# Sixteen graph-network batches on one core: z of eleven batches turned on VectorE and moved by DMA instead of through TensorE

## The chip, the cores and the metric

One NeuronCore of a Trainium2 chip runs the whole program. The metric is the device time of one execution in microseconds (us); lower is better. Engines are named as the profile names them: PE (TensorE matmul), PEld (its weight loads), DVE (VectorE), ACT (ScalarE), POOL (GpSimd), SP (SyncE, which only issues DMAs here).

## What is computed

Sixteen batches `x[b]` of 512 nodes with 128 features go through a two-layer attention network and then through a third attention layer. All arithmetic is fp32. Cut to what matters:

```python
h = relu(layernorm(x))                              # 16 x 512 x 128
o1 = relu(h @ mlp1_w + mlp1_b)                      # 512 x 256 per batch
g1 = gat(o1, None, W_fc, a_fc)                      # attention over all 512 nodes
z = elu(g1) + o1                                    # the residual of the first layer
o2 = relu(z @ mlp2_w + mlp2_b)                      # 512 x 128
g2 = gat(o2, adj, W_hand, a_hand)
x = x + relu(elu(g2) + o2)
x = x + gat(relu(layernorm(x)), adj, W, a)

def gat(inp, adj, W, a):
    h = inp @ W
    e = leaky_relu(h @ a1 + (h @ a2).T)             # 512 x 512
    return elu(softmax(masked(e, adj)) @ h)
```

## The kernel before

**Tiling.** Nodes are cut into C = 4 chunks of 128. The network runs batch by batch, but the batches overlap: every engine has a list `ORDER[engine]` of steps such as `att1_2.7` (attention sums of layer 1, chunk 2, batch 7), which it works off in exactly that order. A step waits on semaphores for its inputs and for its buffers. TensorE's steps fill PSUM banks in rotation: filling number k uses bank k mod 8, and waits until the filling eight before it has been read (`free`, `read_by`).

**The steps of one batch, in the order of the data.** `mlp1_0`, `mlp1_1` (L1416) make o1 by features, that is with features on the partitions and the 512 nodes in the free dimension; ACT puts it into `o1_t` with the ReLU (L790). `h1_0` to `h1_3` (L1426) multiply it with `W_fc`, ACT copies the result to `ext` (L798). DVE finds a column maximum (`max1`, L1138), POOL takes it over the partitions (L732), DVE and ACT make the score factors (`args1`), a row of 512 scores is spread over the partitions (`row1`: DVE turns a 32-wide square, SP writes four small pieces to DRAM at L686 and loads them back as a broadcast at L695), and DVE makes four `prob` tiles of 128x512 (L1184). `att1_0` to `att1_3` (L1437) are the attention sums, one chunk of 128 target nodes each. For each, DVE takes the reciprocal of the row sum (L1250) and ACT scales it to `y` (L892); for each half of the batch ACT then applies exp twice (L911, L915) and DVE forms `u = max(y, min(e, 1))` = elu + 1 (L1265).

**The piece that the change touches.** `u` lies by nodes (nodes on the partitions, 256 features in the free dimension), but `mlp2` needs z by features. So TensorE's steps `z_0` and `z_1` turn it, four 128x128 transposes into one bank each (L1445), and DVE's steps `z_0` and `z_1` (L1272) compute `z_t = (bank - 1) + o1_t`. `mlp2` (L1455) multiplies `z_t` with `mlp2_w`, ACT applies bias and ReLU (L921).

```python
def z(b, f):                       # TensorE, twice per batch
    pe.wait_ge(*s1.u.at(b, 2))
    filled = free(f"z_{f}", b)
    for c in range(C):
        last = nc.tensor.transpose(filled[:, c * P:(c + 1) * P], gat1.u[:, c, f * P:(f + 1) * P], ident[:])
    last.then_inc(z_filled.sem, 1)
```

After `mlp2` come layer 2 (`h2` L1477, `max2`, `args2`, `row2`, `prob2` L859 and L1211, `att2` L1530, `turn_o2` L1538) and layer 3 (`turn2` L1496, `h3` L1477, `max3`, `args3`, `row3`, `prob3`, `att3` L1530). The last three batches (13, 14, 15) run several steps in halves. POOL only takes maxima over the partitions, 16 batches times 3 layers and one guard; it issues no DMA. `o1_t` has 3 buffers, `z_t` has 2.

## Time and profile before

| | us |
|---|---|
| median of 3 runs | 432.97 |
| lowest, highest | 431.36, 433.53 |
| span of the profiled execution | 429.0 |
| PE busy, its share | 411.1, 96% |
| PEld, DVE, ACT busy | 352.7, 357.8, 315.7 |
| POOL busy | 24.9 |

The profile shows one execution of the program and its span from the first to the last instruction. It has no separate time for that execution with what lies around the span; the runs' median is 4.0 us more than the span, the lowest run 2.4 us more. In the profile's rows one fp32 matmul of the program is two MATMUL records (`att1`, 4 matmuls, is "x8"; `att2`, 8 matmuls, is "x16"), and a transpose is one (`z_0` is "x4"). Line numbers are those of the kernel before unless said otherwise. The chain of waits starts from the last instruction and goes back, at each step to what released it; its rows give the share of the span by engine and line. Matmuls are pipelined, so the cost of a step on the chain is the time from its piece to the next piece, not the mean duration of one matmul.

### The profile page before, as it was taken

The page shows a single profiled execution, that of the slowest core. Times are in us where ns is not written, and L with a number is a line of the kernel's source. Part 1 is how long each engine was busy: PE and PEld are TensorE (multiplying, and loading weights), DVE is VectorE, ACT ScalarE, POOL GpSimd, SP SyncE. Part 2 cuts the span into 40 slices and gives each one's busy share as a digit, 9 for nine tenths or more (in the row PEclk, how much of TensorE's full clock was granted, in tenths as well). Part 3 has the DMA queues.
Part 4 walks back from the last instruction along what each step waited for, and adds up shares of the span by engine and source line. Part 5 has one row for each costly group of instructions (what it writes and reads, how often), then busy time and mean ns, then how long its engine had stood idle before and what let it go on. Part 6 is the DMA issues. An engine that isn't in the chain of part 4 may idle for free.

```text
span 429.0 us, 8704 instructions
## 1 busy us (share of the span) xinstructions
PE 411.1 (96%) x2544; PEld 352.7 (82%) x2544; DVE 357.8 (83%) x1226; ACT 315.7 (74%) x764; POOL 24.9 (6%) x53
## 2 busy tenths in 40 slices
PE   6999999999999999999999999999999999989782
PEld 4688779887898899797998788989879799869772
DVE  7786588878998898988898868979698899889974
ACT  2655659658796787786878688687867887799774
POOL 0000000000001000010100000100000000000000
PEclk9999999999999999999999999999999999999997
DMA  7854323123423142232222213222320122120001
GB/s 209 278 146 130 105 74 121 74 76 98 125 98 75 53 138 84 52 101 74 75 82 68 75 53 98 79 72 74 80 87 10 49 93 59 45 80 24 27 1 57
DMA packets 39461, 36.42 MB, mean 85 GB/s; under 512 B 4080, under 2 KB 30320, under 8 KB 39408
## 3 DMA queue, kind: packets, MB, share of 16 engines
q1 hardware_dynamic: 37408, 33.17, 26.1%
q10 hardware_dynamic: 2000, 2.63, 1.8%
q8 instruction: 23, 0.38, 0.4%
q14 instruction: 30, 0.25, 0.2%
HBM read 31.46 MB, written 4.32 MB: 83 GB/s over the span
## 4 chain that ended last, share of the span: by engine, by line
PE 87%; DVE 5%; ACT 3%; issue 2%; DMA 1%; SPq 0%; POOL 0%; ACTq 0%; DVEq 0%
PE bank L1530 24%; PE bank L1437 23%; PE bank L1426 13%; PE bank L1416 6%; PE bank L1477 6%; PE bank L1455 6%; PE bank L1445 3%; PE bank L1538 2%; PE bank L1496 1%; PE bank L1466 1%; DMA row<-row_scratch 1%; DVE stats L1036 1%; DVE u L1265 1%; ACT ext L826 1%; ACT e L911 1%
## 5 line engine op out<-in xcount | busy, mean ns | idle before, releaser
L1530 PEld LDWEIGHTS bank<-ext,prob 128*128 128x128 f32 x1024 | 119.6, 192 | 6.3 <-issue 4.9
L1530 PE MATMUL bank<-ext,prob 128*128 128x129 f32 x1024 | 122.1, 275 | 0.3 <-DVE prob L1207 0.2
L1437 PE MATMUL bank<-ext,prob 128*128 128x257 f32 x512 | 119.0, 380 | 0.0
L1437 PEld LDWEIGHTS bank<-ext,prob 128*128 128x128 f32 x512 | 94.8, 190 | 17.3 <-issue 4.5
L1211 DVE SCALAR_TENSOR_TENSOR prob<-prob,square,mask_t 128x512 f32<-128x512 f32 x98 | 70.6, 739 | 0.9 <-ACT prob L859 0.8
L1426 PE MATMUL bank<-wfc_sb,o_t 128*128 128x259 f32 x256 | 64.0, 382 | 0.4 <-ACT o_t L790 0.4
L859 ACT ACTIVATE prob<-row,square 128x512 f32<-128x512 f32 x78 | 54.1, 720 | 0.1
L1426 PEld LDWEIGHTS bank<-wfc_sb,o_t 128*128 128x128 f32 x256 | 46.3, 190 | 9.6 <-issue 4.5
L903 ACT ACTIVATE y<-bank,recip 128x128 f32<-128x128 f32 x128 | 39.3, 369 | 15.3 <-DVE recip L1257 14.2
L911 ACT ACTIVATE e<-y,minus_one 128x512 f32<-128x512 f32 (+1 forms) x70 | 47.7, 688 | 1.4
L1265 DVE SCALAR_TENSOR_TENSOR u<-e,y 128x512 f32<-128x512 f32 (+1 forms) x70 | 44.1, 638 | 4.2 <-issue 2.2
L732 POOL PARTITION_ALL_REDUCE fmax<-fmax_col x48 | 24.3, 514 | 389.1 <-DVE fmax_col L1138 389.1
L892 ACT ACTIVATE y<-bank,recip 128x256 f32<-128x256 f32 x64 | 29.5, 468 | 16.0 <-DVE recip L1250 15.6
L915 ACT ACTIVATE e<-e,minus_one 128x512 f32<-128x512 f32 (+1 forms) x51 | 35.5, 697 | 2.4
L798 ACT ACTIVATE ext<-bank 128x259 f32<-128x259 f32 x64 | 24.1, 382 | 12.6 <-PE bank L1426 10.6
L1184 DVE TENSOR_SCALAR prob<-row,square 128x512 f32<-128x512 f32 x64 | 32.8, 533 | 0.1
L1416 PE MATMUL bank<-normed_t,w_sb 128*128 128x512 f32 x64 | 32.1, 594 | 0.5 <-DVE normed_t L1097 0.5
L1455 PE MATMUL bank<-z_t,w_sb 128*128 128x512 f32 x64 | 30.2, 594 | 0.0
L790 ACT ACTIVATE o_t<-bank,vec_sb 128x512 f32<-128x512 f32 x32 | 21.7, 682 | 5.4 <-PE bank L1416 4.0
L836 ACT ACTIVATE square<-args 128x12 f32<-128x12 f32 x48 | 10.0, 211 | 18.0 <-DVE args L1159 11.5
L1272 DVE SCALAR_TENSOR_TENSOR z_t<-bank,o_t 128x512 f32<-128x512 f32 x32 | 21.6, 677 | 0.6 <-PE bank L1445 0.2
L826 ACT ACTIVATE ext<-bank,rstd 128x131 f32<-128x131 f32 x64 | 19.1, 378 | 3.2 <-PE bank L1477 2.2
(98 smaller groups left out, 499.1 us busy)
## 6 DMA issues: line engine op xcount, KB each, us to landing
row<-row_scratch SPq DMA_DIRECT2D x36, 256.0 KB, 3.3
moments_row<-moments_scratch SPq DMA_DIRECT2D x13, 512.0 KB, 3.8
x_in<-in_x SPq DMA_DIRECT2D x16, 256.0 KB, 5.3
x_res<-in_x SPq DMA_DIRECT2D x16, 256.0 KB, 4.6
out<-y_out SPq DMA_DIRECT2D x15, 256.0 KB, 3.9
normed<-in_x_t SPq DMA_DIRECT2D x14, 256.0 KB, 4.3
row_scratch<-square_t SPq DMA_DIRECT2D x144, 0.5 KB
adj_sb<-in_adj ACTq DMA_DIRECT2D x1, 1024.0 KB, 8.1
```

Source lines behind the costliest of these rows:

```text
L859: nc.scalar.activation(L.prob_of(b)[:, t], row_of(b, L), ACT.Copy, scale=L.buv[:, b.slot, 2, t:t + 1]).then_inc((s.scaled_first if t == 0 ...
L903: nc.scalar.activation(L.y[:, c], filled[:, e * (D + 3):e * (D + 3) + D], ACT.Copy, bias=1.0, scale=L.recip[:, b.slot, c:c + 1]).then_inc( ...
L911: nc.scalar.activation(L.e[:, r], L.y[:, r], ACT.Exp, bias=minus_one[:]).then_inc(s.exp.sem, 2 // parts)
L915: nc.scalar.activation(L.e[:, r], L.e[:, r], ACT.Exp, bias=minus_one[:]).then_inc(s.exp2.sem, 2 // parts)
L1184: nc.vector.tensor_scalar(gat1.prob_of(b)[:, t], gat1.row[:, b.slot], gat1.buv[:, b.slot, 2, t:t + 1], gat1.buv[:, b.slot, 1, t:t + 1], AL ...
L1211: nc.vector.scalar_tensor_tensor(out=p, in0=p, scalar=L.buv[:, b.slot, 1, t:t + 1], in1=mask_t[:, t], op0=ALU.max, op1=ALU.min).then_inc(s ...
L1265: nc.vector.scalar_tensor_tensor(out=L.u[:, r], in0=L.e[:, r], scalar=1.0, in1=L.y[:, r], op0=ALU.min, op1=ALU.max).then_inc(s.u.sem, 2 // ...
L1416: nc.tensor.matmul(filled[:], w1_sb[:, f * P:(f + 1) * P], normed_t[0][:, b.slot], start=True, stop=True).then_inc(o1_filled.sem, 1)
L1426: last = nc.tensor.matmul(filled[:, 0:H + 3], o1_t[:, b.of(O1_DEPTH), k, c * P:(c + 1) * P], wfc_sb[:, k], start=(k == 0), stop=(k == HT - 1))
L1437: last = nc.tensor.matmul(filled[:, 0:H + 1], gat1.targets(b, t, c), gat1.features_and_one(b, t), start=(t == 0), stop=(t == C - 1))
L1455: last = nc.tensor.matmul(filled[:], w2_sb[:, k], z_t[:, b.slot, k], start=(k == 0), stop=(k == HT - 1))
L1530: last = nc.tensor.matmul(filled[:, e * (D + 3):e * (D + 3) + D + 1], L.targets(b, t, c), L.features_and_one(b, t), start=(t == 0), stop=( ...
```

## The change

For batches 2 to 12 (`MOVED`), z takes another way:

1. TensorE's two `z` steps and DVE's two `z` steps are left out.
2. DVE has two new steps, `turnu_0` and `turnu_1`, each one instruction that turns 32x32 blocks of a half of `u` into `u_turned` (one buffer; the next batch's first `turnu` waits until the writes of the batch before have landed).
3. POOL has a new step `move`: four DMAs, one for each group of 32 partitions, write `u_turned` to a scratch tensor in DRAM, 512 KB per batch in runs of 128 elements (512 bytes).
4. POOL has a new step `move_in`: it waits until those four have landed, then issues one DMA of 128x2x512 elements that reads the scratch and **adds** it onto `o1_t` in place (`accum_op=ALU.add`).
5. `mlp2` reads `o1_t` instead of `z_t`. For the moved batches the 512 nodes lie in `o1_t` in another order, 4 blocks of 4 pieces of 32 nodes; ACT writes them so (`by_blocks`), `mlp2` reads them back in the natural order, in pieces of 32 columns.
6. The "-1" of elu is no longer subtracted by DVE. It goes into the bias: a new step `sums_w2`, once, computes the column sums of `mlp2_w` on TensorE (two matmuls with one column) and DVE subtracts them from `b2_sb`. The five other batches keep their transposes, and their DVE step is a plain add onto `o1_t`.
7. `z_t` is gone, `o1_t` has 4 buffers. Some semaphores that were not used are left out.
8. All five lists in `ORDER` are new.

The diff, cut to its core (the lists of `ORDER` are left out, except POOL's first lines):

```diff
-O1_DEPTH = 3
+O1_DEPTH = 4
+MOVED = tuple(range(2, 13))
...
     "gpsimd": """
-        max1.0 max1.1 max1.2 max2.0 max1.3 max2.1 max1.4 max1.5 max3.0 max2.2 max2.3 max3.1 max2.4 max2.5
+        max1.0 max1.1 max1.2 max2.0 max2.1 max1.3 move.2 move_in.2 max1.4 max1.5 move.3 move_in.3 max3.0 max2.2
+        move.4 max3.1 move_in.4 max2.3 move.5 move_in.5 max2.4 max2.5 max1.6 max1.7 max3.2 max3.3 max1.8 move.6
...
+        u_turned = sb("u_turned", [P, HT * ROWS, C, 32])
+        blocks_scratch = nc.dram_tensor("blocks_scratch", [2, HT * P * N], fp32, kind="Internal").ap()
-        z_t = sb("z_t", [P, 2, HT, N])
...
+        def by_blocks(tile):
+            return tile.rearrange("p (a c i) -> p c a i", a=ROWS, c=C)
...
+            def write_blocks(b):                                     # POOL, "move"
+                pool.wait_ge(*u_blocks.at(b, 2))
+                if b.n - 2 in MOVED:
+                    pool.wait_ge(*z_moved.two_back(b))
+                places = blocks_scratch[b.slot].rearrange("(f j a n) -> a j f n", f=HT * ROWS, j=32, a=ROWS)
+                for a in range(ROWS):
+                    pool.dma_start(places[a], u_turned[32 * a:32 * (a + 1)].rearrange("p f c i -> p f (c i)")).then_inc(
+                        blocks_written.sem(b), 16)
+
+            def add_blocks(b):                                       # POOL, "move_in"
+                pool.wait_ge(*blocks_written.landed(b))
+                pool.wait_ge(*s1.h_filled.at(b, C))
+                pool.dma_start(o1_t[:, b.of(O1_DEPTH)], blocks_scratch[b.slot].rearrange("(k p n) -> p k n", k=HT, p=P),
+                               accum_op=ALU.add).then_inc(z_moved.sem(b), 16)
...
-                nc.scalar.activation(o1_t[:, b.of(O1_DEPTH), f], bank_of(f"mlp1_{f}", b)[:], ACT.Relu,
-                                     bias=b1_sb[:, f:f + 1]).then_inc(o1_ready.sem, 1)
+                o1, filled = o1_t[:, b.of(O1_DEPTH), f], bank_of(f"mlp1_{f}", b)[:]
+                if moved(b):
+                    o1, filled = by_blocks(o1), filled.rearrange("p (c a i) -> p c a i", a=ROWS, c=C)
+                nc.scalar.activation(o1, filled, ACT.Relu, bias=b1_sb[:, f:f + 1]).then_inc(o1_ready.sem, 1)
...
+            def turn_blocks(b, part):                                # DVE, "turnu"
+                r = slice(part * C // 2, (part + 1) * C // 2)
+                dve.wait_ge(*s1.u.at(b, part + 1))
+                earlier = [n for n in MOVED if n < b.n]
+                if part == 0 and earlier:
+                    dve.wait_ge(*blocks_written.landed(Batch.nth(earlier[-1])))
+                nc.vector.transpose(u_turned[:, :, r].rearrange("p f c i -> p c f i"),
+                                    gat1.u[:, r].rearrange("p c (f i) -> p c f i", i=32)).then_inc(u_blocks.sem, 1)
...
-                nc.vector.scalar_tensor_tensor(out=z_t[:, b.slot, f], in0=bank_of(f"z_{f}", b)[:], scalar=-1.0,
-                                               in1=o1_t[:, b.of(O1_DEPTH), f], op0=ALU.add, op1=ALU.add).then_inc(
-                    z_ready.sem, 1)
+                o1 = o1_t[:, b.of(O1_DEPTH), f]
+                nc.vector.tensor_tensor(o1, bank_of(f"z_{f}", b)[:], o1, ALU.add).then_inc(z_ready.sem, 1)
...
             def mlp2(b):                                             # TensorE
-                pe.wait_ge(*z_ready.at(b, HT))
+                pe.wait_ge(*(z_moved.landed(b) if moved(b) else z_ready.at(b, HT)))
                 filled = free("mlp2", b)
                 for k in range(HT):
-                    last = nc.tensor.matmul(filled[:], w2_sb[:, k], z_t[:, b.slot, k],
+                    z = o1_t[:, b.of(O1_DEPTH), k]
+                    last = nc.tensor.matmul(filled[:], w2_sb[:, k], by_blocks(z) if moved(b) else z,
                                             start=(k == 0), stop=(k == HT - 1))
```

**What the new order does, at two places.** The first is TensorE around batch 4. Before, from `h3_0.1` to `mlp2.4`; L1445 are the `z` transposes, first those of batch 4 and between them `att1_2.5` (L1437), and the last row is `mlp2.4`:

```order
L1477 MATMUL bank<-wl_sb,normed_t 128x131 x4
L1477 MATMUL bank<-whand_sb,o_t 128x131 x4
L1416 MATMUL bank<-normed_t,w_sb 128x512
L1437 MATMUL bank<-ext,prob 128x257 x8
L1416 MATMUL bank<-normed_t,w_sb 128x512
L1445 MATMUL bank<-ident,u 128x128 x4
L1437 MATMUL bank<-ext,prob 128x257 x4
L1445 MATMUL bank<-ident,u 128x128 x4
L1530 MATMUL bank<-ext,prob 128x129 x8
L1437 MATMUL bank<-ext,prob 128x257 x4
L1426 MATMUL bank<-wfc_sb,o_t 128x259 x2
L1455 MATMUL bank<-z_t,w_sb 128x512 x2
```

After, from `mlp2.3` (first row) to `mlp2.4` (last row). In the changed kernel L1518 is `mlp2`, L1499 `att1`, L1561 `turn2`, L1542 `h2` or `h3`, L1595 `att3`, L1478 `mlp1`. Just ahead of the first row stand the four `att1` steps of batch 4 and the four transposes of `row3.0`:

```order
L1518 MATMUL bank<-o_t,w_sb 128x512 x2
L1561 MATMUL bank<-ident,normed 128x128 x4
L1499 MATMUL bank<-ext,prob 128x257 x8
L1542 MATMUL bank<-wl_sb,normed_t 128x131 x4
L1542 MATMUL bank<-whand_sb,o_t 128x131 x2
L1499 MATMUL bank<-ext,prob 128x257 x4
L1542 MATMUL bank<-whand_sb,o_t 128x131 x2
L1499 MATMUL bank<-ext,prob 128x257 x4
L1595 MATMUL bank<-ext,prob 128x129 x8
L1478 MATMUL bank<-normed_t,w_sb 128x512
L1595 MATMUL bank<-ext,prob 128x129 x8
L1518 MATMUL bank<-o_t,w_sb 128x512 x2
```

The transposes are gone. `mlp2.4` comes after `att1_3.5` and both `att3` steps of batch 0.

The second place is POOL in the changed kernel, from `max2.3` (first row) to `move_in.8` (last row); L744 is a maximum over the partitions, L754 the four writes of a `move`, L761 the adding DMA of a `move_in`. Before, POOL's list was maxima alone:

```order
L744 ISA fmax<-fmax_col 128x1
L754 DMA blocks_scratch<-u_turned 32x8x128 x4
L761 DMA o_t<-blocks_scratch 128x2x512
L744 ISA fmax<-fmax_col 128x1 x7
L754 DMA blocks_scratch<-u_turned 32x8x128 x4
L761 DMA o_t<-blocks_scratch 128x2x512
L744 ISA fmax<-fmax_col 128x1 x2
L754 DMA blocks_scratch<-u_turned 32x8x128 x4
L761 DMA o_t<-blocks_scratch 128x2x512
L744 ISA fmax<-fmax_col 128x1 x4
L754 DMA blocks_scratch<-u_turned 32x8x128 x4
L761 DMA o_t<-blocks_scratch 128x2x512
```

Maxima now stand behind the waits of `move` and `move_in` on the same engine; ahead of `move.7` (the third L754) are `max2.6` and `max3.4`, and ahead of `move.8` are `max1.9`, `max3.5`, `max2.7` and `max1.10`.

## Rows read from the trace of the kernel before

**Rows 1.** The page: busy time of each engine, share of the span, instructions

```profile
PE 411.1 (96%) x2544; PEld 352.7 (82%) x2544; DVE 357.8 (83%) x1226; ACT 315.7 (74%) x764; POOL 24.9 (6%) x53
```

**Rows 2.** The page: chain of waits, shares of the span by engine and line

```profile
PE 87%; DVE 5%; ACT 3%; issue 2%; DMA 1%; SPq 0%; POOL 0%; ACTq 0%; DVEq 0%
PE bank L1530 24%; PE bank L1437 23%; PE bank L1426 13%; PE bank L1416 6%; PE bank L1477 6%; PE bank L1455 6%; PE bank L1445 3%; PE bank L1538 2%; PE bank L1496 1%; PE bank L1466 1%; DMA row<-row_scratch 1%; DVE stats L1036 1%; DVE u L1265 1%; ACT ext L826 1%; ACT e L911 1%
```

**Rows 3.** Windows: us, busy PE, PEld, DVE, ACT, POOL, then granted clock, DMA share, GB/s

```profile
0.00:30.00 30.00, 25.46 (x118) 19.55 (x119) 23.57 (x119) 13.74 (x32) 1.11 (x6) 1.00 0.74 219
30.00:60.00 30.00, 30.00 (x147) 23.92 (x146) 21.17 (x85) 19.27 (x45) 1.27 (x3) 1.00 0.37 107
...
330.00:360.00 30.00, 30.00 (x198) 26.87 (x197) 26.83 (x88) 23.30 (x60) 1.81 (x5) 1.00 0.19 59
360.00:390.00 30.00, 28.21 (x193) 24.74 (x192) 25.68 (x82) 26.70 (x63) 2.22 (x4) 1.00 0.19 57
390.00:429.00 39.00, 27.40 (x227) 25.30 (x225) 30.03 (x100) 27.14 (x73) 1.05 (x3) 0.93 0.10 30
```

**Rows 4.** The chain of waits from 190 us on: start us, us, what

```profile
190.29 1.73 PE bank L1437 x8
...
192.90 0.86 PE bank L1416 x2
...
194.63 0.44 PE bank L1445 x4
...
198.65 1.79 PE bank L1455 x4
...
202.17 0.89 PE bank L1477 x8
203.07 0.88 PE bank L1426 x4
...
207.44 1.78 PE bank L1530 x16
```

**Rows 5.** Groups of instructions: busy us, mean ns of one | idle before

```profile
L1265 DVE SCALAR_TENSOR_TENSOR u<-e,y 128x512 f32<-128x512 f32 x58 | 39.3, 684 | 4.0 <-issue 2.2 <-ACT e L915 1.3 <-ACT e L911 0.6
...
L1184 DVE TENSOR_SCALAR prob<-row,square 128x512 f32<-128x512 f32 x64 | 32.8, 533 | 0.1
L915 ACT ACTIVATE e<-e,minus_one 128x512 f32<-128x512 f32 x45 | 32.5, 722 | 2.2
...
L892 ACT ACTIVATE y<-bank,recip 128x256 f32<-128x256 f32 x64 | 29.5, 468 | 16.0 <-DVE recip L1250 15.6 <-DVE u L1265 0.2
...
L1272 DVE SCALAR_TENSOR_TENSOR z_t<-bank,o_t 128x512 f32<-128x512 f32 x32 | 21.6, 677 | 0.6 <-PE bank L1445 0.2
...
L1445 PE MATMUL bank<-ident,u 128*128 128x128 f32 x128 | 18.5, 273 | 1.7 <-DVE u L1265 1.7
...
L1129 DVE TENSOR_SCALAR normed<-x,meanvar 128x128 f32<-128x128 f32 x64 | 14.3, 282 | 0.7
...
L1369 PE MATMUL bank<-vec_sb,turned_w 128*128 128x3 f32 x8 | 1.0, 242 | 0.0
```

**Rows 6.** DMA issues on SP from 238 us on: start us, us, what

```profile
238.29 1.28 SPq L663 DMA_DIRECT2D moments_scratch<-moments_t  x4
241.31 0.35 SPq L668 DMA_DIRECT2D moments_row<-moments_scratch  x1
...
249.97 1.06 SPq L675 DMA_DIRECT2D x_res<-in_x  x1
```

**Rows 7.** DMA issues: KB each, median us from issue to landing

```profile
moments_row<-moments_scratch SPq DMA_DIRECT2D x13, 512.0 KB, 3.8
...
out<-y_out SPq DMA_DIRECT2D x15, 256.0 KB, 3.9
...
adj_sb<-in_adj ACTq DMA_DIRECT2D x1, 1024.0 KB, 8.1
```

More of the change, by code:

```diff
@@ L66 @@
+        move.4 max3.1 move_in.4 max2.3 move.5 move_in.5 max2.4 max2.5 max1.6 max1.7 max3.2 max3.3 max1.8 move.6
+        move_in.6 max2.6 max3.4 move.7 move_in.7 max1.9 max3.5 max2.7 max1.10 move.8 move_in.8 max3.6 move.9 max2.8
+        move_in.9 move.10 max2.9 move_in.10 max1.11 max3.7 max2.10 max1.12 max3.8 max1.13 move.11 max3.9 move_in.11
+        move.12 move_in.12 max2.11 max2.12 max3.10 max1.14 max2.13 max1.15 max3.11 max3.12 max2.14 max3.13 max2.15
+        max3.14 max3.15 guard
     """,
@@ new lines @@
+        norm1.5 prob1_0.1 prob1_1.1 prob1_2.1 prob1_3.1 stats1.7 norm1.6 elu1_0.0 elu1_1.0 att1_0.1 z_0.0 stats1.8
+        att1_1.1 z_1.0 normt.4 att1_2.1 max1.2 att1_3.1 args1.2 elu1_0.1 elu1_1.1 max2.0 args2.0 z_0.1 z_1.1
+        prob1_0.2 prob1_1.2 prob1_2.2 prob1_3.2 prob2_0.0 max2.1 max1.3 args2.1 prob2_1.0 args1.3 row1.3 att1_0.2
+        att1_1.2 att1_2.2 att1_3.2 prob2_2.0 prob2_3.0 norm1.7 normt.5 prob1_0.3 prob1_1.3 att2_0.0 att2_1.0
+        prob1_2.3 elu1_0.2 normt.6 prob1_3.3 turnu_0.2 norm1.8 elu2.0 att1_0.3 elu1_1.2 stats1.9 prob2_0.1 att1_1.3
@@ L219 @@
+        att1_0.15 turn_o2.13 att1_1.15 z_1.14 att1_2.15 att1_3.15 mlp2.14 turn2.13 h2_0.14 h2_1.14 h3_0.13 h3_1.13
+        z_0.15 z_1.15 att3_0.12 row2.14 mlp2.15 row3.13 att3_1.12 h2_0.15 h2_1.15 att2_0.14 att2_1.14 turn_o2.14
+        row2.15 att3_0.13 att3_1.13 att2_0.15 att2_1.15 turn_o2.15 turn2.14 h3_0.14 h3_1.14 row3.14 turn2.15 h3_0.15
+        h3_1.15 att3_0.14 row3.15 att3_1.14 att3_0.15 att3_1.15
     """,
@@ L475, in gnn_program @@
         o1_ready = signal("o1_ready", HT)
-        z_filled = signal("z_filled", HT)
-        z_ready = signal("z_ready", HT)
+        unmoved = [n for n in range(B) if n not in MOVED]
+        u_blocks = signal("u_blocks", 2, without=unmoved)
+        blocks_written = slots("blocks_written", unmoved, ROWS)
+        z_moved = slots("z_moved", unmoved)
+        z_filled = signal("z_filled", HT, without=MOVED)
+        z_ready = signal("z_ready", HT, without=MOVED)
         o2_filled = signal("o2_filled", 1)
@@ L683, in write_row @@
                     sp.wait_ge(*s.row_loaded.two_back(b))
-                rows = L.scratch[b.slot].rearrange("(c k i) -> k c i", c=C, k=ROWS)
+                order = "(k c i) -> k c i" if L is gat1 and moved(b) else "(c k i) -> k c i"
+                rows = L.scratch[b.slot].rearrange(order, c=C, k=ROWS)
                 for k in range(ROWS):
@@ L744, in pool_steps @@
                 "guard": guard_over_partitions,
+                "move": write_blocks,
+                "move_in": add_blocks,
             }
@@ L1378, in score_columns23, with sums_w2 @@
                                             start=True, stop=True)
+                last.then_inc(s_waf, 1)
+            def sums_w2(b):
+                pe.wait_ge(s_w2, 16)
+                filled = free("sums_w2", b)
+                for k in range(HT):
+                    last = nc.tensor.matmul(filled[:, 0:1], w2_sb[:, k], score_scale[:, 1, 0:1],
+                                            start=(k == 0), stop=(k == HT - 1))
                 last.then_inc(s_waf, 1)
@@ L1464, in spread_row @@
                 pe.wait_ge(*s.buv.at(b, 1))
+                places = filled[:].rearrange("p (c n) -> p c n", c=C)
+                if L is gat1 and moved(b):
+                    places = filled[:].rearrange("p (c a i) -> p a c i", a=ROWS, c=C)
                 for c in range(C):
-                    last = nc.tensor.transpose(filled[:, c * P:(c + 1) * P],
-                                               L.buv[:, b.slot, 0, c:c + 1].broadcast_to([P, P]), ident[:])
+                    last = nc.tensor.transpose(places[:, c], L.buv[:, b.slot, 0, c:c + 1].broadcast_to([P, P]), ident[:])
                 last.then_inc(s.row_filled.sem, 1)
```

341 lines of the change are left out of this document (166 added, 175 removed).

## The prediction

> **What bounds the kernel now.** I read the busy times first, then the chain of waits, then windows along the span. PE is busy 411.1 of 429.0 us; DVE has 357.8, ACT 315.7, POOL 24.9 [rows 1]. PE makes 87% of the chain that ended last, DVE 5%, ACT 3%; the z transposes (L1445) alone are 3% of it [rows 2]. The windows say where PE rests: in the first 30 us it is busy 25.46, from 30 to 360 us every window reads 30.00 of 30.00 (two of the eleven are shown), then 28.21 of 30 and 27.40 of the last 39 [rows 3]. So for 330 us nothing but PE's own queue sets the time, at a granted clock of 1.00: work taken from PE there is time gained, as long as no wait takes its place.
>
> **What is removed.** On the chain one z step (four transposes, L1445 x4) takes 0.44 us [rows 4]. I take this price and not the 273 ns of one transpose [rows 5], since the transposes overlap. 11 batches times 2 steps: 22 x 0.44 = **9.7 us** off PE, all of it inside the stretch in which PE never rests.
>
> **What costs little.** DVE loses 22 adds of 677 ns and gets 22 block turns of 128x512. No such turn is in the trace; the nearest rows of that shape are 533 ns (L1184) and 684 ns (L1265) [rows 5], so DVE changes by -3 to +0.2 us, beside PE. The new column sums are two small matmuls, four records; eight such records (L1369) are busy 1.0 us [rows 5]: +0.5 on PE. The bias and the five unmoved batches change nothing by count. `mlp2` reads its moving side in pieces of 32 columns; its price is now 1.79 us per batch [rows 4], and I take it unchanged, since the same 512 columns go through. The bound above is twice that, 11 x 1.79 = 19.7 us.
>
> **The new wait.** For a moved batch `mlp2` waits for a path that leaves PE: last attention sum `att1_3`, then ACT and DVE to both halves of `u`, the turn, POOL's four writes and their landing, POOL's add and its landing. What hides it is the PE work queued between `att1_3` and `mlp2` of that batch. I priced PE's new list with the chain's steps: `att1` 1.73, `mlp1` 0.86, `mlp2` 1.79, `h2` or `h3` 0.44 a half, `h1` 0.88, `att2` or `att3` 1.78, transposing steps as z 0.44 [rows 4] (L1477 x8 is both halves of a batch, L1426 x4 is one `h1`). Between `att1_3` and `mlp2` then stand 15.8 us for batch 4 (the place shown), 17.1 for 12, 17.2 for 10, 18.1 for 5, 19.7 for 11, and 22.3 to 25.0 for the other six.
>
> The path, in three parts:
> - *To the turned u.* Below: one `y` 0.47, two exps 0.72 each, `u` 0.68, a turn 0.68 [rows 5] = 3.3 us. Above: in the old list 6.2 us of PE work stood between `att1_3.10` and `z_0.10`, and PE did not rest there [rows 3], so `u` was ready by then; with a turn 6.9. DVE and ACT queues are well filled, so I take 5.5, nearer the upper end.
> - *The writes, W.* Below: SP issues four small pieces and the load that waits for them starts 3.0 us after the first (238.29 to 241.31) [rows 6]. Above: four issues like the dearest on SP, 1.06 [rows 6], and the landing of a 256 KB store, 3.9 [rows 7] = 8.1. Three issues at the middle of 0.32 and 1.06, 2.1, and a landing of 2.9 between those of the small pieces (1.7 after the last issue) and of the store give 5.0.
> - *The add, A.* Below: a plain load of 512 KB, 3.8. Above: the 1024 KB of the adjacency, 8.1 [rows 7], as the add moves each byte in and also reads the destination. I take the middle, 6.0.
>
> So W + A = **11 us, between 6.8 and 16.2**, and the path is 16.5. Only batch 4 is short, by 0.7 us; 10 and 12 have 0.6 to spare.
>
> *POOL as a queue.* Maxima and moves stand on one engine. `move.7` stands behind `max2.6`, whose input comes 7.5 us of PE work after `att1_3.7`; with the copy and the maxima it issues at about 8.8 instead of 5.5, and 8.8 + 11 = 19.8 is under 22.3. `move.8` goes at 10.2 (behind `max2.7`) and ends at 21.2 of 23.8. `move_in.9` stands behind `max2.8`, at 14.6, and ends at 20.6 of 22.4. `move.11` goes at 7.1 and ends at 18.1 of 19.7. In the other direction, `max1.9` behind `move_in.7` is not late: 15.7 us of PE work come before its input is there. These reserves are 1.6 to 2.6 us, so this cover is gone once W + A passes about 12.6.
>
> **The sum.** -9.7 + 0.5 + 0.7 = -8.5. What the new lists do elsewhere, at the start (4.5 us of rest), in the last 39 us (11.6 us of rest) [rows 3] and where moves crowd the row loads, no row separates; I take +1, between -2 and +4. That is -7.5, a span of 421.5. The runs' median is 4.0 over the profiled span, so against it 432.97 - 7.5 = **425.5 us**.
>
> The Trainium skill (DMA: Bandwidth & Descriptors, section on the anatomy of a DMA on the gpsimd path) gives about 2.0 us plus bytes at 436 GB/s per DMA: an estimate of 2.3 us for a write and 3.2 for the add, under my values; by it no batch is short and the time is about 424.8. No DMA issued on POOL is in the trace before, so nothing here shows it yet.
>
> **The rivals.**
> 1. *POOL's DMAs are held up by DVE, and the gain is mostly given back.* For it: DVE is busy 83% [rows 1], and its TENSOR_SCALAR form goes from 282 ns for 128 columns to 533 for 512, 0.65 ns a column, faster than the 684 ns of a two-input form [rows 5], so it may use something that POOL needs too. Against: nothing on POOL is seen to wait for it. If each of the five DMAs of a batch waits one such instruction, W + A = 11 + 5 x 0.53 = 13.7. Then batch 4 waits 3.4, 10 waits 2.0, 11 and 12 together 2.1, 7 waits 0.2: 7.7 in all, and the time is 432.97 - 9.2 + 7.7 + 1 = **432.5**. This mechanism is the one of the Trainium skill (SBUF — State Buffer, section on the two separate sides): while DVE runs an operation on both ports, GpSimd cannot write the descriptors of its DMAs.
> 2. *Slower: POOL's DMA path is longer than its cover.* Place: `mlp2` of the moved batches, PE idle there. Beyond W + A = 13.8 the waits (8.2) outweigh the gain, and from there each us costs some 5, since batches 4, 10, 12, 7 and 9 then wait each (batch 5, 8 and 11 have another's wait inside their own window). At 16, near the upper bound, they wait 5.7, 4.3, 4.4, 2.4 and 1.6 = 18.5: 432.97 - 9.2 + 18.5 + 1 = **443 us**. For it: five DMAs in series with two landings, on an engine that never issued one, with an add that touches its data twice. Against: the load of 512 KB lands in 3.8 [rows 7], and DMA engines are only a fifth to a third busy in the middle [rows 3].
> 3. *The change doesn't save what the steps cost*: reading `o1_t` in pieces slows `mlp2`, or DVE (83%) and ACT take PE's place. Half the bound of the piecewise read, 9.8 us, gives 425.5 + 9.8 = **about 435**. Against: neither DVE nor ACT gets more work.
>
> **How the numbers follow.** Forecast 0.60 (421.5 to 430.2; the upper end is W + A = 13, where waits are 5.4), rival 1 0.14, rival 2 0.19, rival 3 0.07. The forecast is all faster; rival 1 is 0.02 faster and 0.12 same; rival 3 is 0.03 same and 0.04 slower; rival 2 is slower. That makes faster 0.62, same 0.15, slower 0.23, with 0.5% (2.2 us) as about what a measurement can tell from no change. The range is 421.5 to 437: it holds the forecast, rivals 1 and 3 and the near part of rival 2 (W + A up to about 14.8), and leaves out some 0.15.
>
> **What would show it.** L1445 at 40 records instead of 128. POOL's rows: the first write to the landing of the last about 5 us, the add about 6. PE still without rest from 30 to 350 us but for about 1 us at `mlp2.4`; `mlp2` still 1.79 us on the chain; block turns between 0.53 and 0.68 us. Rival 1 shows as POOL issues with gaps that end with DVE instructions. Rival 2 shows as PE idle at `mlp2`, released by the adding DMA, in five or more batches. I am wrong if PE rests over 6 us in the middle, or if it does not and the time still stays above 430.

## The result: slower, 446.6 us, and the profile after

The changed kernel takes 446.64 us in the median of 4 runs (445.68 to 449.04), the kernel before 432.79 (431.36 to 433.53) beside it on the same chip. The ratio is 1.034, with a 95% interval of 1.030 to 1.038: 14 us slower, where 7.5 us faster was forecast, and outside the range. The profiled execution took 447.09 us, its span is 445.2. Medians count all executions and ratios only the fast ones, so in runs 4 and 9, which have slow ones among them, the two do not quite agree. Each run below has the kernel before measured beside it (medians 431.7 to 432.7 us).

The page of the changed kernel: busy times, the queue of GpSimd's DMAs (packets, MB, share of the 16 DMA engines), then the chain of waits by engine.

```profile
PE 408.6 (92%) x2460; PEld 344.9 (77%) x2460; DVE 358.1 (80%) x1227; ACT 314.2 (71%) x764; POOL 63.8 (14%) x108
...
q0 software_dynamic: 5104, 11.54, 13.4%
...
issue 29%; PE 26%; DVE 11%; DMA 7%; POOL 5%; ACT 2%; SPq 1%; POOLq 0%; DVEq 0%; ACTq 0%
```

PE made 87% of the chain [rows 2] and makes 26% now. Its busy time fell by only 2.5 us, where 9.7 us of steps had gone [rows 1]. The windows show where it rests (columns as in [rows 3]):

```profile
90.00:120.00 30.00, 27.86 (x151) 22.01 (x149) 23.41 (x90) 21.25 (x53) 9.09 (x14) 1.00 0.64 155
120.00:150.00 30.00, 23.62 (x144) 19.00 (x145) 19.64 (x59) 17.34 (x42) 5.03 (x8) 0.94 0.51 128
150.00:180.00 30.00, 30.00 (x199) 27.07 (x199) 28.24 (x94) 24.29 (x63) 1.95 (x4) 1.00 0.32 87
...
300.00:330.00 30.00, 27.23 (x152) 22.50 (x151) 23.39 (x64) 20.89 (x49) 9.06 (x13) 0.94 0.51 123
330.00:360.00 30.00, 30.00 (x181) 25.14 (x181) 23.76 (x82) 23.42 (x58) 2.17 (x5) 1.00 0.26 62
```

From 90 to 330 us PE is busy 220.6 of 240 us (eight windows, four of them shown); it never rested there before. It rests where POOL's moves are: 150:180 and 330:360, with no move issued in them, read 30.00.

Groups of the changed kernel: busy us, mean ns of one | idle before it and what ended that. L892 and L1224 build the `prob` tiles from the row of scores that is broadcast through DRAM; L1518 is `mlp2`, L754 the four writes of a move.

```profile
L892 ACT ACTIVATE prob<-row,square 128x512 f32<-128x512 f32 x78 | 52.6, 717 | 14.4 <-DMA row<-row_scratch 14.4
...
L1518 PE MATMUL bank<-o_t,w_sb 128*128 128x512 f32 x64 | 34.0, 656 | 16.8 <-DMA o_t<-blocks_scratch 16.7
...
L1224 DVE TENSOR_SCALAR prob<-row,square 128x512 f32<-128x512 f32 x64 | 32.1, 541 | 5.5 <-DMA row<-row_scratch 5.2
...
L754 POOL DMA_DIRECT2D blocks_scratch<-u_turned x44 | 26.4, 616 | 55.7 <-DVE u_turned L1319 55.5
```

Two new waits stand here. PE waits 16.7 us for the adding DMA (nine times, at most 4.8). And ACT and DVE wait for the row load, L892 14.4 us and L1224 5.2, with 7.2 more at a third line (L1233); no such wait of any size was in the trace before. The DMA issues say what the new transfers take from issue to landing (KB each, median us):

```profile
blocks_scratch<-u_turned POOLq DMA_DIRECT2D x44, 128.0 KB, 2.9
o_t<-blocks_scratch POOLq DMA_DIRECT2D x11, 512.0 KB, 6.1
```

The longest wait, batch 5, in the timeline (start us, us, what [idle before it and its end]):

```profile
131.88 1.23 POOL L761 DMA_DIRECT2D o_t<-blocks_scratch  x1 [5.68 <-DMA blocks_scratch<-u_turned]
...
136.63 1.44 SPq L698 DMA_DIRECT2D row_scratch<-square_t  x4
...
140.27 3.67 PE L1518 MATMUL bank<-o_t,w_sb 128*128 128x512 f32 x4 [4.81 <-DMA o_t<-blocks_scratch]
...
141.86 0.34 SPq L707 DMA_DIRECT2D row<-row_scratch  x1
```

The add is issued at 131.88 and landed at 140.23. In the same stretch SP writes a row (136.63) and can issue its load only at 141.86, 5.2 us later. `mlp2` then takes 3.67 us, where the same row reads 1.98 at most of the other moved batches (the 1.79 of [rows 4] counts from piece to piece): after its rest of 4.81 us PE ran these matmuls at half pace, up to 1222 ns against a median of 592, and the window reads a granted clock of 0.94, which is part of it at the lower of the levels of 1.2 and 2.4 GHz. The same shows at batch 11 (a wait of 2.77 us, then 3.14 for `mlp2`). It does not show at batch 7, where PE waited 3.12 us and `mlp2` took 1.98, so the length of the last rest does not decide it alone.

### The profile page after: what moved, and what is told of

The parts are those of the page before. It is cut to its first block, busy times and chain, and to the rows that moved or that the text cites. A ratio compares the mean times of both kernels' runs of the same rounds, so it can differ in the third digit from the quotient of the medians.

```text
span 445.2 us, 8586 instructions
## 1 busy us (share of the span) xinstructions
PE 408.6 (92%) x2460; PEld 344.9 (77%) x2460; DVE 358.1 (80%) x1227; ACT 314.2 (71%) x764; POOL 63.8 (14%) x108
## 3 DMA queue, kind: packets, MB, share of 16 engines
q0 software_dynamic: 5104, 11.54, 13.4%
## 4 chain that ended last, share of the span: by engine, by line
issue 29%; PE 26%; DVE 11%; DMA 7%; POOL 5%; ACT 2%; SPq 1%; POOLq 0%; DVEq 0%; ACTq 0%
PE bank L1595 10%; PE bank L1499 6%; DMA o_t<-blocks_scratch 5%; PE bank L1518 3%; POOL blocks_scratch L754 3%; PE bank L1542 3%; POOL fmax L744 2%; DVE prob L1251 2%; DVE u_turned L1319 2%; PE bank L1488 2%; DVE stats L1076 1%; DMA row<-row_scratch 1%; DVE u L1305 1%; PE bank L1478 1%; DMA moments_scratch<-moments_t 1%
## 5 line engine op out<-in xcount | busy, mean ns | idle before, releaser
L1595 PEld LDWEIGHTS bank<-ext,prob 128*128 128x128 f32 x1024 | 119.1, 192 | 6.9 <-issue 5.6
L1595 PE MATMUL bank<-ext,prob 128*128 128x129 f32 x1024 | 121.4, 275 | 0.5 <-DVE prob L1251 0.3
L1499 PE MATMUL bank<-ext,prob 128*128 128x257 f32 x512 | 116.5, 382 | 1.8 <-DVE prob L1224 1.8
L1499 PEld LDWEIGHTS bank<-ext,prob 128*128 128x128 f32 x512 | 95.5, 191 | 19.2 <-issue 5.7
L744 POOL PARTITION_ALL_REDUCE fmax<-fmax_col x48 | 24.8, 530 | 282.1 <-DVE fmax_col L1178 282.0
L892 ACT ACTIVATE prob<-row,square 128x512 f32<-128x512 f32 x78 | 52.6, 717 | 14.4 <-DMA row<-row_scratch 14.4
L1488 PE MATMUL bank<-wfc_sb,o_t 128*128 128x259 f32 x256 | 60.7, 382 | 0.4 <-ACT o_t L824 0.4
L1488 PEld LDWEIGHTS bank<-wfc_sb,o_t 128*128 128x128 f32 x256 | 47.6, 190 | 10.4 <-issue 4.0
L1518 PE MATMUL bank<-o_t,w_sb 128*128 128x512 f32 x64 | 34.0, 656 | 16.8 <-DMA o_t<-blocks_scratch 16.7
L936 ACT ACTIVATE y<-bank,recip 128x128 f32<-128x128 f32 x128 | 37.6, 370 | 11.2 <-DVE recip L1297 10.6
L925 ACT ACTIVATE y<-bank,recip 128x256 f32<-128x256 f32 x64 | 28.0, 469 | 18.0 <-DVE recip L1290 17.8
L1224 DVE TENSOR_SCALAR prob<-row,square 128x512 f32<-128x512 f32 x64 | 32.1, 541 | 5.5 <-DMA row<-row_scratch 5.2
L1518 PEld LDWEIGHTS bank<-o_t,w_sb 128*128 128x128 f32 x64 | 11.9, 200 | 29.1 <-DMA o_t<-blocks_scratch 20.0
L754 POOL DMA_DIRECT2D blocks_scratch<-u_turned x44 | 26.4, 616 | 55.7 <-DVE u_turned L1319 55.5
L1478 PE MATMUL bank<-normed_t,w_sb 128*128 128x512 f32 x64 | 31.3, 594 | 0.6 <-DVE normed_t L1137 0.6
L956 ACT ACTIVATE o_t<-bank,vec_sb 128x512 f32<-128x512 f32 x16 | 11.0, 685 | 22.4 <-PE bank L1518 22.4
L824 ACT ACTIVATE o_t<-bank,vec_sb 128x512 f32<-128x512 f32 x32 | 21.3, 684 | 4.5 <-PE bank L1478 4.5
```

What stands on the lines that cost most here:

```text
L754: pool.dma_start(places[a], u_turned[32 * a:32 * (a + 1)].rearrange("p f c i -> p f (c i)")).then_inc(blocks_written.sem(b), 16)
L892: nc.scalar.activation(L.prob_of(b)[:, t], row_of(b, L), ACT.Copy, scale=L.buv[:, b.slot, 2, t:t + 1]).then_inc((s.scaled_first if t == 0 ...
L936: nc.scalar.activation(L.y[:, c], filled[:, e * (D + 3):e * (D + 3) + D], ACT.Copy, bias=1.0, scale=L.recip[:, b.slot, c:c + 1]).then_inc( ...
L1478: nc.tensor.matmul(filled[:], w1_sb[:, f * P:(f + 1) * P], normed_t[0][:, b.slot], start=True, stop=True).then_inc(o1_filled.sem, 1)
L1488: last = nc.tensor.matmul(filled[:, 0:H + 3], o1_t[:, b.of(O1_DEPTH), k, c * P:(c + 1) * P], wfc_sb[:, k], start=(k == 0), stop=(k == HT - 1))
L1499: last = nc.tensor.matmul(filled[:, 0:H + 1], gat1.targets(b, t, c), gat1.features_and_one(b, t), start=(t == 0), stop=(t == C - 1))
```

## The experiments

The question was which of three things cost 14 us: the new lists, the wait at `mlp2`, or the transfers themselves. Runs 1, 2, 5 to 8 and 11 leave the elu of layer 1 out of batches 2 to 12, so what they compute is not the result; they are read for their time alone. Runs 3, 4, 9, 10 and 12 compute all of it.

### 1. Without the moves

All `move` and `move_in` steps are left out of POOL's list, and DVE's turn no longer waits for writes to land. In `mlp2` (cut):

```
-pe.wait_ge(*(z_moved.landed(b) if moved(b) else z_ready.at(b, HT)))
+if not moved(b):
+    pe.wait_ge(*z_ready.at(b, HT))
```

> The changed kernel without move and move_in: no DMA on POOL, and mlp2 of batches 2 to 12 waits for nothing and reads o1 alone (elu of layer 1 is left out of those batches, their bias is unshifted). Turns and all lists stay. Theory T (the loss is the wait at mlp2, whose path begins late because u is turned 6 to 17 us after att1_3, plus the lower clock after such waits): PE does not rest in the middle, 423 to 426 us. Rival L (the new lists themselves are worse, whatever the DMAs do): over 430. Rival C (POOL's DMAs crowd the row loads) expects 423 to 426 here too.

Measured: **423.5 us**, ratio to the kernel before 0.981 (0.977 to 0.985). Waits of PE from 40 to 385 us (total us, times, longest), and the new kind of wait on ACT:

```profile
PE bank L1564 <- DVE normed L1174: 0.7, 1, 0.7
PE bank L1490 <- ACT o_t L828: 0.6, 1, 0.6
...
ACT prob L896 <- DMA row<-row_scratch: 8.5, 8, 2.8
```

The new lists and the 22 steps saved give 8 to 9 us, as the forecast of the steps had it. But ACT waits 8.5 us for row loads, without any move, where the trace before shows no such wait: in the new lists some rows come too late already.

### 2. All transfers, but nobody waits for them

```
-pool.dma_start(o1_t[:, b.of(O1_DEPTH)], blocks_scratch..., accum_op=ALU.add)
+pool.dma_start(aside[:], blocks_scratch..., accum_op=ALU.add)
```

and no wait at `mlp2`, as above. (Also new are one clearing of `aside` at the start, and each add waits for the one before it to land.)

> All DMAs of the change run, but the adding DMA adds onto a tile that nobody reads, so mlp2 of batches 2 to 12 waits for none of them (layer 1's elu is left out of these batches as in the run without DMAs). Theory T: 423 to 427, at most 2 above the run without DMAs. Rival C: 430 or more, 5 to 15 above the run without DMAs, with ACT and DVE waiting for row loads.

Measured: **439.04 us**, ratio 1.015 (1.010 to 1.020). So the wait at `mlp2` that the trace puts at 16.7 us is worth 446.6 - 439.0 = 7.6 us; the other 15.5 us (439.0 - 423.5) come from transfers that nobody waits for. By the intervals of the two runs, each of these shares is good to about 3 us either way (an estimate). From 90 to 330 us PE rests 0.6 us in run 1, 12.8 in run 2 and 19.4 in the changed kernel. The row waits that grew (the one other wait of ACT or DVE for a DMA, for a load of x, is 3.4 us, once):

```profile
ACT prob L907 <- DMA row<-row_scratch: 22.9, 11, 4.6
DVE prob L1249 <- DMA row<-row_scratch: 13.6, 6, 4.9
...
DVE prob L1240 <- DMA row<-row_scratch: 4.1, 2, 3.2
```

The row path in both timelines, first with the transfers (SP, then POOL), then without. `row_scratch<-square_t` are the four small writes of 0.5 KB, `row<-row_scratch` the load of 256 KB that waits for them to land:

```profile
183.22 2.55 SPq L706 DMA_DIRECT2D row_scratch<-square_t  x4
189.80 0.35 SPq L715 DMA_DIRECT2D row<-row_scratch  x1
...
183.55 1.24 POOL L775 DMA_DIRECT2D aside<-blocks_scratch  x1 [3.37 <-issue]
```

```profile
174.00 1.60 SPq L702 DMA_DIRECT2D row_scratch<-square_t  x4
176.57 0.35 SPq L711 DMA_DIRECT2D row<-row_scratch  x1
```

The same row: 6.6 us from the first write to the load with an add issued beside it, 2.6 without. Over all 36 rows, those whose writes meet an add in flight (counted from 1 us after its issue to its landing, against the 2 us after the first write) had a mean of 4.3 us in this run (10 rows), the 21 that met no move 2.5. Their loads also landed later: 4.0 against 3.5 us.

### 3 and 4. Two tries with the lists

The first puts z back onto TensorE in all batches, with two z steps about 3 us of PE work ahead of each `mlp2` in the new lists, and DVE's two adds in place of its turns (the tensor list is cut to one stretch):

```
-MOVED = tuple(range(2, 13))
+MOVED = ()
-... h1_3.5 turn_o2.2 mlp1_1.7 att2_0.3 mlp2.5
+... h1_3.5 z_0.5 z_1.5 turn_o2.2 mlp1_1.7 att2_0.3 mlp2.5
```

> The new lists, but z of all batches goes through TensorE as before (two transposing steps 3 us of PE work ahead of each mlp2, two adds on DVE; no move, no move_in). Theory T: as much as before, 431 to 435. Rival L: 438 or more.

Measured: 454.05 us, ratio 1.049 (1.043 to 1.055). PE waits at `mlp2` for the DVE add of z:

```profile
PEld bank L1522 <- DVE o_t L1329: 11.9, 6, 3.5
PE bank L1522 <- DVE o_t L1329: 9.5, 5, 3.1
```

Where the z steps stand was my choice, and a poor one, so this says nothing of the lists; experiment 1 does.

The second brings the turned `u` forward: VectorE's and ScalarE's steps between `att1` and the turn stand as early as their inputs allow (a stretch of the vector list).

```
-elu1_0.5 max2.3 args3.1 row3.1 args2.3 turnu_0.5 att1_3.5
+elu1_0.5 prob3_1.0 att1_2.5 turnu_0.5 max3.1 prob3_2.0 prob3_3.0 att1_3.5 max2.3
```

> The changed kernel with the lists of DVE and ACT rewritten for batches 2 to 12 alone: reciprocals, y, exps, u and turns of layer 1 stand where they can run right after their att1 step, so that the turn ends about 4 to 5 us after att1_3 instead of 6 to 17. Theory T: the waits at mlp2 fall from 16.8 to under 4 us and the time to 428 to 434. Rivals C and L: it stays over 441.

Measured: 455.46 us, ratio 1.050 (1.040 to 1.059). A miss, and a telling one. The turn now ends 5.0 to 8.4 us after `att1_3`, 6.6 in the mean instead of 10.8, and the wait that it aims at does shrink, from 16.7 to 6.1 us. Others take its place (PE from 40 to 385 us, then ACT, whose wait for `recip` was 17.8 us in the changed kernel):

```profile
PE bank L1523 <- DMA o_t<-blocks_scratch: 6.1, 5, 2.6
PE bank L1600 <- DVE prob L1256: 4.7, 10, 2.0
...
ACT y L930 <- DVE recip L1295: 40.5, 32, 3.7
```

As I read it, DVE and ACT have no room of their own in these lists: what goes first makes something else late.

### 5 to 7. Which transfers, bytes or issues

All three start from run 2 (nobody waits for the transfers). The first keeps every issue and wait of POOL and cuts the bytes to an eighth:

```
-pool.dma_start(places[a], u_turned[32 * a:32 * (a + 1)]...)
+pool.dma_start(places[a][:, 0:1], u_turned[32 * a:32 * (a + 1), 0:1]...)
-pool.dma_start(aside[:], blocks_scratch...)
+pool.dma_start(aside[0:32, 0:1], blocks_scratch...[0:32, 0:1])
```

> As in the run without the wait at mlp2 (439.0 us): all 55 transfers are issued by GpSimd at the same places, with the same waits of its queue, and nobody waits for them, but each carries an eighth of its bytes and packets (16 KB for a write, 64 KB for an add; so z is left out of the eleven moved batches, as there). Theory of traffic (the small row writes and the row loads are slowed by the bytes and packets that the moves put into the 16 DMA engines): 423 to 428 us, the row loads again issued 2.1 to 3.5 us after their row writes, as without any move, and not up to 6.6 us. Rival (GpSimd's own work and queue: its 55 issues, its waits and the maxima behind them, or its descriptor writing that disturbs VectorE): 437 to 440 us. In between: both.

The second leaves the adds out (no `move_in` steps):

> As in the run without the wait at mlp2 (439.0 us), but only the 44 writes of 128 KB are issued and the eleven adds are left out, with GpSimd's wait for the landing (z is left out of the moved batches). If the writes (704 packets' worth of 512 bytes each batch and more) carry the crowding: 434 to 439 us. If the adds carry it: 424 to 428 us. If both do by their bytes (the same bytes each): about 431 us.

The third issues the writes for two batches alone:

```
-for a in range(ROWS):
+for a in range(ROWS if b.n in MOVED[:2] else 0):
```

> The counterpart: as in the run without the wait at mlp2 (439.0 us), but the writes are issued for batches 2 and 3 alone, and the eleven adds of 512 KB at their places, some 5 us earlier since they wait for no landing (z is left out of the moved batches). If the adds carry the crowding: 434 to 439 us. If the writes do: 424 to 428 us. By bytes: about 432 us. Together with writes only: the excesses over 423.5 us should add to about 15.5 us if the two act alike on the rows; much less would say that the effect needs both.

Measured: an eighth **424.84 us** (ratio 0.984, 0.980 to 0.988), writes only **425.66** (0.984, 0.980 to 0.989), adds only **440.18** (1.018, 1.015 to 1.022). POOL's 55 issues, its waits and the maxima behind them are 1.3 us over run 1 together, and the 44 writes with their issues 2.2; both lie within the intervals, so they are small and not clear of the noise. The adds cost nearly all of it, with the same bytes as the writes. The row waits, writes only and then adds only:

```profile
ACT prob L906 <- DMA row<-row_scratch: 10.7, 6, 3.4
```

```profile
ACT prob L907 <- DMA row<-row_scratch: 26.4, 9, 5.5
DVE prob L1249 <- DMA row<-row_scratch: 12.2, 8, 3.6
```

### 8 and 9. Is it the adding, and can POOL add instead

Run 2 again, with the 512 KB as a plain load:

```
-pool.dma_start(aside[:], blocks_scratch..., accum_op=ALU.add)
+pool.dma_start(aside[:], blocks_scratch...)
```

> As in the run without the wait at mlp2 (439.0 us: 44 writes and eleven adds of 512 KB, which nobody waits for), but the eleven 512 KB transfers only copy from DRAM into the tile beside, without adding (z is left out of the moved batches). Theory A (it is the adding, which has to read what it adds onto, that holds up the row writes: the adds took 52 us of DMA-engine time each, the four writes with the same bytes 31 us, and the writes alone cost 2 us): 424 to 429 us, landing in 3.5 to 4.5 us instead of 6.1, as the 512 KB moments load (3.8 us), and row loads that start 2.1 to 3.9 us after their row writes. Theory B (any 512 KB read from DRAM onto SBUF just there does it): 436 to 441 us, with row loads up to 5 or 6.6 us after their writes.

Measured: **430.06 us**, ratio 0.995 (0.992 to 0.997), between the two theories. The plain load lands in 4.4 us. DMA queue (packets, MB, share), then the landing:

```profile
q0 software_dynamic: 3696, 11.54, 9.1%
...
aside<-blocks_scratch POOLq DMA_DIRECT2D x11, 512.0 KB, 4.4
```

The same queue with the writes alone (run 6), and with adds alone (run 10 below):

```profile
q0 software_dynamic: 2112, 5.77, 5.1%
```

```profile
q0 software_dynamic: 2992, 5.77, 8.6%
```

By the shares of q0, eleven adds and 44 writes take 13.4% of 16 engines for 441.3 us = 946 us of engine time, eleven plain loads and the writes 9.1% of 16 x 428.8 = 624, the writes alone 345 (5.1% of 16 x 423.2). An add is then 55 us of engine time, a plain load of the same bytes 25; run 10, with no other DMAs on this queue, gives 54. The packets say where that time goes: an add has 272 (2992 / 11), a plain load 144 ((3696 - 2112) / 11), so a packet takes 0.20 us in an add and 0.18 in a plain load. (A write has 48, 2112 / 44; the 704 in my expectation for run 6 is not what a batch has.) Less the writes' 2.2, the plain loads cost 4.4 us, the adds 13.3.

The version of the whole computation that this suggests, a plain load into a tile of its own and the addition on POOL (cut):

```
+nc.gpsimd.tensor_tensor(o1_t[:, b.of(O1_DEPTH)], o1_t[:, b.of(O1_DEPTH)], z_in[:], op=ALU.add)
```

> The whole result is computed. As the changed kernel, but the 512 KB transfer is a plain load into a tile of its own, and GpSimd adds that tile onto the first-layer output with one tensor_tensor of 128x1024; mlp2 waits for that. By theory A the crowding of the rows (15.5 us) mostly goes, and the path from the turned u is writes 5.2 + load 3.8 to 4.5 + the add, whose duration no run shows (1 to 3 us as an estimate between VectorE's 0.7 us for half as many elements and three times that for a full tile): 10 to 12.7 against 11.2 to 12.6 now, so the stall at mlp2 stays near 7 us: 423.5 + 2 + 7 = 431 to 434 us, level with the kernel before. By theory B 444 to 450 us, level with the changed kernel. Rival: GpSimd's add and VectorE's instructions hold each other up; then both take longer and the time is above 440 us by that alone, with longer means in VectorE's groups.

Measured: **560.55 us**, ratio 1.294 (1.287 to 1.302). None of the theories had this, and not the rival either: the instructions of VectorE are no longer than in the changed kernel (742 ns against 743 in the mean of its costliest group). PE waits 49.6 us at `mlp2` for POOL's add and DVE 39.7 for the maxima behind it, and the windows of 30 us between 90 and 210 us read a granted clock of 0.66 to 0.77, with a mean of 925 ns for a matmul of `mlp2`. POOL's timeline around one batch:

```profile
179.95 0.75 POOL L770 DMA_DIRECT2D z_in<-blocks_scratch  x1 [3.45 <-DMA blocks_scratch<-u_turned]
189.25 2.33 POOL L776 TENSOR_TENSOR o_t<-o_t,z_in 128x1024 f32<-128x1024 f32 x1 [8.55 <-issue]
197.55 0.38 POOL L752 PARTITION_ALL_REDUCE fmax<-fmax_col  x1 [5.98 <-issue]
```

The add itself is 2.3 us, but POOL stands still for 8.6 us before it, of which the landing of the load (4.6 us after its issue) explains 3.9, and for 6.0 us before the next maximum, whose input was there. The queue of POOL shows one more thing, at the line of the add:

```profile
L776 POOLq MODIFY_POOL_CONFIG  x20: 37/37/37, 85.4 to 420.3; - x20
```

Each change between this kind of instruction and the maximum comes with such a step. The Trainium skill (GPSIMD Engine Reference, section on instruction dispatch) says that the first call of a newly loaded GpSimd kernel pays about 6 us for loading its code, with no instruction in the profile; the 6.0 us before the maximum and the 4.7 left before the add are of that size. That this is the cause is not shown: no run separates it.

### 10 and 11. Does it matter where the adds fall, and in which lists

Run 11 is run 6 (writes only), with eleven adds of input data put back, each held until a chosen row load has landed with 5 to 18 us of silence on the row path behind it:

```
+pool.wait_ge(*sig[L].row_loaded.landed(Batch.nth(n)))
+pool.dma_start(aside[:], x[b.n:b.n + 2]..., accum_op=ALU.add)
```

> The run with the writes alone (425.7 us) and eleven adds of 512 KB put back beside it: they add two batches of the input onto a tile that nobody reads, and each waits until a chosen row load has landed after which the row path (row write, row load) is idle for 5 to 18 us, instead of following its own batch's writes (z is left out of the moved batches, nobody waits for the adds). If the adds cost because they fall on row writes and row loads (10 of 36 row writes lay under an add in the run at 439.0, and their loads started 4.3 us after them, not 2.5): 425 to 430 us. If an add costs whatever lies beside it (DMA engines busy, GpSimd's issue of 1.2 us, memory ports of the engines): 437 to 441 us.

Measured: 434.91 us, ratio 1.005 (1.003 to 1.008): between the theories. Most of the gaps that I chose are 5 to 7 us long and the adds took 5.5 to 9, so five rows still met an add instead of ten. With half of the collisions the adds cost 9.2 us over run 6, against 13.3 for those of run 2. So the time does not fall in step with the rows that meet an add. Part of the rest is of this run's own making: its plain writes landed later too (a median of 3.6 us, 2.9 in run 6), seven rows met them alone, with a mean of 3.5 us, and DVE once waited 3.4 us for `u_turned` to be written out.

Run 10 is the kernel before, with eleven such adds when z of batches 2 to 12 is added:

```
+pool.wait_ge(*z_ready.at(b, HT))
+pool.dma_start(aside[:], x[b.n:b.n + 2]..., accum_op=ALU.add)
```

> The kernel before (all z through TensorE, its own lists), with eleven adds of 512 KB of the input onto a tile that nobody reads, issued by GpSimd when z of batches 2 to 12 is added. The whole result is computed. In the kernel before no engine's wait of any size is released by a row load, while the run without transfers has 8.5 us of such waits on ScalarE already: if the rows in the lists before have slack (the new lists are what makes them late), 433 to 437 us. If the adds cost the same 15 us in any list: 446 to 449 us.

Measured: **433.60 us**, ratio 1.002 (1.000 to 1.005): about 1 us, where eleven adds cost 13 to 17 in the new lists. The rows are held up here too, one row by 3.4 us more (SP's timeline of this run, then of the kernel before):

```profile
118.03 1.54 SPq L686 DMA_DIRECT2D row_scratch<-square_t  x4
124.78 0.34 SPq L695 DMA_DIRECT2D row<-row_scratch  x1
```

```profile
114.94 1.28 SPq L686 DMA_DIRECT2D row_scratch<-square_t  x4
118.26 0.34 SPq L695 DMA_DIRECT2D row<-row_scratch  x1
```

but hardly anybody waits for them (3.4 us in sum, the largest on DVE 1.6):

```profile
ACT prob L872 <- DMA row<-row_scratch: 1.5, 3, 0.8
```

So the harm has two halves: the adds delay rows in either kernel, and in the new lists more of the rows are due when they come. How much belongs to each is not separated, since the delay itself is smaller here: nine rows met an add, with a mean of 3.3 us from the first write to the load against 2.3 for the other 27, about 1 us each, where ten rows of run 2 had about 1.8.

### 12. The version that this points to

The new code with the lists of the kernel before, and only the three batches moved that have the longest time from `u` to `mlp2`:

```
-MOVED = tuple(range(2, 13))
+MOVED = (2, 3, 8)
-mlp2.2 h1_3.5 turn_o2.1
+h1_3.5 turn_o2.1 mlp2.2
-mlp2.8 att1_0.10
+att1_0.10 mlp2.8
```

> The whole result is computed. The changed kernel's code with the lists of the kernel before, in which eleven adds cost 1.2 us, and only batches 2, 3 and 8 moved: those with the longest time from the finished u to mlp2 in the trace before (11.4, 15.2 and 11.6 us; the others 3.6 to 9.2). mlp2 of batch 2 stands 1.3 us of TensorE's work later, that of batch 8 1.7 us. Theory (a batch pays where the 12.3 us of turn, writes and add are covered and the rows have slack): 3 x 0.88 = 2.6 us saved, stalls at mlp2 of about 0.9 and 1.5 us for batches 2 and 8, none for 3, 0.3 us for the adds beside: about 432.4 - 2.6 + 2.4 + 0.3 + 0.5 (sums_w2) = 433, 431 to 434 us, level with the kernel before. Rival: the first-layer output is now kept until mlp2 has read it, since the sum is made in place; in lists that were not made for it, mlp1 waits for it and the time is above 436 us.

Measured: 438.14 us, ratio 1.012 (1.009 to 1.015). Slower than forecast and than the kernel before, though the adds are hardly waited for:

```profile
PEld bank L1523 <- DMA o_t<-blocks_scratch: 0.5, 2, 0.3
```

Yet PE rests 4.7 us from 30 to 360 us by the windows, where it had not rested at all, in small pieces of at most 1.7 us that end with DVE's and ACT's steps. No wait of size names the kept first-layer output, the rival. Which of the three batches, or the turns in DVE's list, costs most was not separated. No version here beats the kernel before.

## Where the 14 us come from

All runs of the new lists side by side. "Row waits" is the sum of what ACT and DVE wait for `row<-row_scratch` in each profile, which is one execution; that of run 2 took 443.1 us, above its median.

| run | moves | time us | over run 1 | row waits us |
|---|---|---|---|---|
| 1 | none | 423.5 | 0 | 9.9 |
| 5 | all issues, 1/8 of the bytes | 424.8 | 1.3 | 10.4 |
| 6 | writes | 425.7 | 2.2 | 12.9 |
| 8 | writes, plain loads | 430.1 | 6.6 | 18.3 |
| 11 | writes, adds in gaps | 434.9 | 11.4 | 22.0 |
| 2 | writes, adds | 439.0 | 15.5 | 40.6 |
| 7 | adds, early, and the writes of two batches | 440.2 | 16.7 | 42.2 |
| changed kernel | writes, adds, and `mlp2` waits | 446.6 | 23.1 | 26.8 |

Where nobody waits for a move, time and row waits rise in the same order. In the changed kernel the row waits are smaller than in run 2. As I read it, part of that lateness is spent while PE stands at `mlp2`, and so a wait shown as 16.7 us gives back only 7.6; PE's rest from 90 to 330 us falls by 6.6 with it, not by 16.7. The sum: 432.8 - 9.3 (lists and steps) + 15.5 (transfers, nearly all adds) + 7.6 (the wait) = 446.6.

What makes an add hold up a small row write stays open. In run 2 the load of the row started within 0.4 us of the add's landing at six of the ten rows that met one. The delay is larger with the transfer of more engine time (4.3 us for the ten rows of run 2, 3.0 for the ten that met a plain load in run 8; 55 and 25 us of engine time for the same bytes). The Trainium skill (DMA: Bandwidth & Descriptors, section on queues, rings and completion order) says that each DMA engine goes round its queues packet by packet, finishing a packet of one before it serves the next. By that rule longer packets would keep SP's small writes waiting longer. If the profile's packets are those of the page, the rows do not bear this out: those of an add take 0.20 us each and those of a plain load 0.18, and what differs is their number, 272 and 144. Run 5 points the same way: its adds have an eighth of the bytes, in packets of 2 KB as before, and the eight rows that met one had a mean of 2.7 us, near the 2.4 of the others. So the number of packets, or the time for which they keep the engines busy, goes with the delay, and not the length of one; how it holds up a row write is not shown.

## The prediction, step by step

- **Where PE rests, and the price of the steps** ([rows 3, 4]): right. Run 1 gives 8.3 us by its ratio and 9.3 by its medians, against -9.7 + 0.5 + 1 = -8.2. The piecewise read of `mlp2` costs nothing (592 ns is its median matmul), and a block turn is 704 ns, just above the 0.68 taken as bound.
- **Writes and add, W + A = 11**: near, and somewhat low. From the first write to the add it is 4.9 to 8.0 us, 5.2 in the median, and from the add to its landing 6.0 to 8.4; the sum is 10.9 to 13.3 in ten of eleven batches, and 16.4 in batch 5, just past the bound of 16.2 and at the longest wait. Its mean is 12.4. POOL's write issues take 582 to 763 ns each with DVE 80% busy, and no gap of them ends with VectorE other than the wait for `u_turned` itself, so rival 1 (VectorE holds up POOL's descriptors; the Trainium skill, SBUF — State Buffer, section on the two separate sides) shows no trace. The Trainium skill (DMA: Bandwidth & Descriptors, section on the anatomy of one DMA) gave 2.3 and 3.2 us by estimate; 2.9 for a write is near, 6.1 for the add is about twice it.
- **POOL as a queue**: hardly put to the test. The turned `u` came so late that the maxima listed ahead of the moves held none of them up by much: in every batch the first write is issued 0.3 to 0.9 us after the turn.
- **To the turned `u`, 5.5, at most 6.9**: wrong. From the end of `att1_3` it is 6.2 to 16.7 us, 10.8 in the mean of eleven batches. The bound was taken from one batch, 10, which is the shortest of all (6.2). In the trace before `u` was ready 4.3 to 14.7 us after `att1_3`; that could be read batch by batch, and I read one. This is the first step that failed, and the one that made "only batch 4 is short" fall: PE waited at nine of eleven batches, 16.7 us in sum against 0.7 (worth 7.6 in the kernel's time).
- **Rival 2** named this (adding DMA in five or more batches), but put it on W + A above 13.8. Its time, 443, is near; its cause was the other part of the path.
- **"Where moves crowd the row loads, no row separates; I take +1, between -2 and +4"**: the second step that failed, and the larger error: 15.5 us. The effect was named and then priced without a row. The rows that bear on it were there: an add was taken to touch its data twice (A between 3.8 and 8.1), and a row needs 2.3 us and 3.5 us of small and medium DMAs on the same engines. What no row of before could show is the other half, that the new lists leave some rows no slack (ACT waits 8.5 us for them with no move at all); the slack belongs to the lists, and its trace did not exist yet. From the order alone, the distance from each row's write to its first user could have been compared in both lists.
- "I am wrong if PE rests over 6 us in the middle": it rests 19.4 from 90 to 330 us, and the clause came true.
